# State-space layers of a perceiver block reordered along the next program's chain, one bias matmul of 256 columns, and a buffer cleared in two pieces elsewhere

## The reference, cut to what matters

```python
xz = x @ in_w
u, z = jnp.split(xz, 2, axis=-1)
uc = cb + sum((up[:, k:k + L, :] * cw[:, k] for k in range(D_CONV)))   # up: u padded in time
u = jax.nn.silu(uc)
proj = u @ xpw                       # dt (8), B (16), C (16)
delta = jax.nn.softplus(dt @ dtw + dtb)
h = exp(delta * A) * h + (delta * u) * B_t      # a scan over time, 16 states per channel
y = sum_n(h * C_t) + u * D
y = y * jax.nn.silu(z)
x = layer_norm(y @ ow + x)           # four layers, one after the other
```

## Time and profile before

| | us |
|---|---|
| median of 3 runs | 709.41 (709.27 to 709.52) |
| the profiled execution | 708.04 |
| its span, first to last instruction | 706.2 |
| busy in the span: TensorE, VectorE, ScalarE, POOL | 574.1, 478.9, 299.5, 161.7 |
| state-space layers, from the first turning (L1686) | 480.2 to 689 |

### The profile page before, as it was taken

How to read it: one execution, slowest core, us unless ns; L and a number is a source line. 1 busy time by engine, 2 the same in 40 slices (tenths; PEclk the granted TensorE clock), 3 DMA queues, 4 the chain that set the end, 5 groups by cost and what they waited for, 6 DMA issues and landing times.

```text
span 706.2 us, 21667 instructions
## 1 busy us (share of the span) xinstructions
PE 574.1 (81%) x8501; PEld 449.5 (64%) x8501; DVE 478.9 (68%) x1894; ACT 299.5 (42%) x851; POOL 161.7 (23%) x208
## 2 busy tenths in 40 slices
PE   3958758569995699999899999886788988898866
PEld 2625534357884688888888888875456656665634
DVE  1568649964444677777777777771588888978783
ACT  2868725224565333333233233233545444555411
POOL 2245533117000000000000000001564356336600
PEclk9989979796997555555555555555799999999997
DMA  8800000010002000000000000000000000000000
GB/s 341 354 1 2 1 3 1 2 41 3 1 1 90 3 3 0 0 0 0 0 0 0 0 0 0 0 1 0 1 0 1 1 0 1 1 0 1 1 0 7
DMA packets 6057, 15.26 MB, mean 22 GB/s; under 512 B 2641, under 2 KB 3289, under 8 KB 5505
## 3 DMA queue, kind: packets, MB, share of 16 engines
q1 hardware_dynamic: 5296, 11.19, 4.3%
q10 hardware_dynamic: 720, 3.55, 1.3%
HBM read 14.60 MB, written 0.13 MB: 21 GB/s over the span
## 4 chain that ended last, share of the span: by engine, by line
PE 41%; DVE 33%; ACT 13%; issue 10%; DMA 1%; DVEq 1%; POOL 0%; SPq 0%; ACTq 0%; POOLq 0%
PE bank L1678 9%; PE bank L1751 7%; PE bank L1587 6%; ACT esp L676 3%; PE bank L1538 2%; DVE ssum L1138 2%; ACT a L662 2%; DVE T L1208 2%; ACT e L678 2%; PE bank L1525 2%; DVE rz L1175 2%; DVE zs L1173 2%; DVE asp L1128 2%; DVE opre L1114 2%; ACT T L546 1%
## 5 line engine op out<-in xcount | busy, mean ns | idle before, releaser
L472 POOL MEMSET ctxT<- 128x128 f32 x1 | 0.3, 312 | 305.8 <-DVE xres L1182 305.8
L1587 PE MATMUL bank<-esp,qblk 128*128 128x1 f16 (+1 forms) x2048 | 66.5, 166 | 0.8 <-ACT esp L676 0.8
L1587 PE MATMUL bank<-hsp,kT 128*128 128x2 f16 x2048 | 63.5, 166 | 2.3 <-DVE hsp L1166 1.7
L1587 PEld LDWEIGHTS bank<-esp,qblk 128*128 128x128 f16 x2048 | 61.2, 104 | 1.4 <-ACT esp L676 1.1
L662 ACT ACTIVATE a<-opre 128x4 f32<-128x4 f32 x64 | 13.1, 205 | 115.2 <-DVE opre L1126 115.2
L1587 PEld LDWEIGHTS bank<-hsp,kT 128*128 128x128 f16 x2048 | 59.9, 104 | 3.1 <-DVE hsp L1163 1.7
L1208 DVE SCALAR_TENSOR_TENSOR T<-bank,bct,T 128x256 f32<-128x256 f32 x112 | 46.4, 476 | 1.3 <-PE bank L1764 1.3
L1195 DVE TENSOR_TENSOR_SCAN qblk<-ctxT,bank 128x512 f32<-128x512 f32 x32 | 37.6, 1208 | 13.2 <-PE bank L1751 13.2
L1587 PE MATMUL bank<-asp,lsp 128*128 128x4 f16 x768 | 30.7, 168 | 16.3 <-DVE asp L1128 16.3
L1195 DVE TENSOR_TENSOR_SCAN w<-kT,bank 128x512 f32<-128x512 f32 x32 | 37.6, 1208 | 8.4 <-PE bank L1751 8.4
L1587 PEld LDWEIGHTS bank<-asp,lsp 128*128 128x128 f16 x768 | 25.4, 105 | 27.8 <-DVE asp L1128 27.7
(11 more groups left out here) (326 smaller groups left out, 1410.5 us busy)
## 6 DMA issues: line engine op xcount, KB each, us to landing
w<-in_w_dram SPq DMA_DIRECT2D x2, 2048.0 KB
ctxT<-in_ctxT_dram SPq DMA_DIRECT2D x8, 256.0 KB, 13.4
wqkv<-in_qkvT_dram ACTq DMA_DIRECT2D x1, 1536.0 KB, 12.2
w<-in_mw_dram SPq DMA_DIRECT2D x1, 1024.0 KB, 5.1
lw<-in_lw_dram SPq DMA_DIRECT2D x1, 960.0 KB, 19.8
rows<-in_rows_dram ACTq DMA_DIRECT2D x1, 772.0 KB, 8.2
wqkv<-in_fw_dram SPq DMA_DIRECT2D x1, 532.0 KB, 3.4
T<-in_mask_dram ACTq DMA_DIRECT2D x1, 512.0 KB, 6.2
```

What stands on the lines that cost most here:

```text
L1587: return pe.matmul(out, lhsT, rhs, start=start, stop=stop, skip_group_check=True)
```

## The change

Four things. (1) POOL clears three quarters of `qblk` as its first instruction and the first quarter right after the cross-attention's last scaling, instead of all of it after L432; VectorE waits for both. (2) The two bias matmuls of 128 columns become one of 256 columns, at both places, and the one for the softplus' argument moves ahead of its input's wait. (3) The input projection is split: the u half goes before the convolution, the z half after it and after one bank of turned states; the sigmoid of u comes before that of z; the copy of bct moves behind the first exponential of the softplus; `turned_x` and the padded copy move ahead of the decays 5 to 7. (4) In each period, `sum_y` moves behind scan input 1, `project_out` between scan inputs 2 and 3, scan input 7 behind two banks of turned states; VectorE's scan 7 goes behind three read-outs and `gated_u`, and eight read-outs stand behind du instead of six; POOL waits for delta only, not for du.

```diff
--- POOL
+            pool.memset(qblk[:, 1:XG, :, :, :], 0.0).then_inc(sem["a_zero"], 1)
             pool.wait_ge(sem["d_mask"], 16)
...
             for i in range(B * XG):
...
+            pool.wait_ge(sem["x_max"], B * XG)
+            pool.memset(qblk[:, 0, :, :, :], 0.0).then_inc(sem["a_zero"], 1)
             pool.wait_ge(sem["a_wmean"], 1)
...
-            pool.memset(qblk[:, :, :, :, :], 0.0).then_inc(sem["a_zero"], 1)
...
-                pool.wait_ge(sem["m_delta"], 2 * c + 2)
+                pool.wait_ge(sem["m_delta"], 2 * c + 1)
--- ScalarE, prepare(c), new order
+                act.wait_ge(sem["m_uc"], c + 1)
+                step(act.activation(m_eu, bank[5][:, 0:TOK], ACT.Exp, scale=-1.0))
+                step(act.activation(m_lu, m_eu, ACT.Ln, bias=one))
+                act.activation(m_sg, m_lu, ACT.Exp, scale=-1.0).then_inc(sem["m_sig"], 1)
                 act.wait_ge(sem["m_uz"], 2 * c + 2)
                 step(act.activation(m_eu, bank[6][:, 0:TOK], ACT.Exp, scale=-1.0))
...
-                step.mark(act.activation(m_abs, bank[4][:, 0:TOK], ACT.Abs))
+                step(act.activation(m_abs, bank[4][:, 0:TOK], ACT.Abs))
                 act.wait_ge(sem["m_p"], 2 * c + 2)
+                step.mark(act.activation(bank[7][:, TOK:2 * TOK], m_abs, ACT.Exp, scale=-1.0))
                 act.activation(bct[:, s, :], bank[7][:, 0:2 * MN], ACT.Copy).then_inc(sem["m_bcs"], 1)
                 step.sync()
-                act.wait_ge(sem["m_bcs"], c + 1)
-                step(act.activation(bank[7][:, TOK:2 * TOK], m_abs, ACT.Exp, scale=-1.0))
--- ScalarE, period
                 decays(q, 0, 5)
                 if q >= 1:
                     rstd(q - 1)
-                decays(q, 5, 7)
                 if c:
                     turned_x(c)
-                decays(q, 7, NT)
+                decays(q, 5, 6)
+                if c:
+                    padded_u(c)
+                decays(q, 6, NT)
                 if c:
                     prepare(c)
--- VectorE
-                dve.wait_ge(sem["a_zero"], 1)
+                dve.wait_ge(sem["a_zero"], 2)
...
-                for i in range(3, NT):
+                for i in range(3, 7):
                     scan(q, i)
+                read_out(q, 0, 2)
                 if c:
                     gated_u(c)
+                read_out(q, 2, 3)
+                scan(q, 7)
+                if c:
                     gated_z(c)
-                read_out(q, 0, 7)
+                read_out(q, 3, 6)
                 if c:
                     ratio(c)
-                read_out(q, 7, 10)
+                read_out(q, 6, 8)
                 if c:
                     first_factor(c)
                     steps_of_time(c)
-                read_out(q, 10, MN)
+                read_out(q, 8, MN)
--- TensorE
-            def bias(to, n, start):
-                return mm(to, biasT[:, :], pat(cst[0:2 * ML * MC, C_ID + n:C_ID + n + 1], [[0, P]]), start=start)
+            def biases(to, n):
+                return mm(to[:, 0:TOK], biasT[:, :], pat(cst[0:2 * ML * MC, C_ID + n:C_ID + n + 1], [[1, MC], [0, P]]), start=True)
...
-                if q:
-                    scan_input(q, 0, 1)
-                    sum_y(q - 1)
-                    scan_input(q, 1, 4)
-                    project_out(q - 1)
-                else:
-                    scan_input(q, 0, 4)
-                scan_input(q, 4, 6)
+                scan_input(q, 0, 2)
+                if q:
+                    sum_y(q - 1)
+                scan_input(q, 2, 3)
+                if q:
+                    project_out(q - 1)
+                scan_input(q, 3, 6)
                 if c:
                     turned(c)
                 scan_input(q, 6, 7)
                 if c:
-                    project_in(c)
+                    project_in(c, 0)
                     convolve(c)
+                turn_state(q, 0, 1)
+                if c:
+                    biases(bank[4], ML * MC + c // 2 * MC)
+                    project_in(c, 1)
+                turn_state(q, 1, 2)
                 scan_input(q, 7, 8)
-                turn_state(q, 0, 2)
                 if c:
                     project_u(c)
                 turn_state(q, 2, 8)
```

More of the change, by code:

```diff
@@ L710, in turned_x, with padded_u @@
                 act.activation(m_xT[c % 2], bank[5][:, 0:P], ACT.Copy).then_inc(sem["m_xp"], 1)
+            def padded_u(c):
+                act.wait_ge(sem["m_uz"], 2 * c + 1)
+                act.activation(upad[:, c % 2, :, :, MK - 1:], bank[4][:, 0:TOK].rearrange("p (c b t) -> p c b t", c=MC, b=BT),
+                               ACT.Copy).then_inc(sem["m_up"], 1)
             def prepare(c):
                 s = c % 2
-                act.wait_ge(sem["m_uz"], 2 * c + 1)
-                act.activation(upad[:, s, :, :, MK - 1:], bank[4][:, 0:TOK].rearrange("p (c b t) -> p c b t", c=MC, b=BT),
-                               ACT.Copy).then_inc(sem["m_up"], 1)
+                act.wait_ge(sem["m_uc"], c + 1)
+                step(act.activation(m_eu, bank[5][:, 0:TOK], ACT.Exp, scale=-1.0))
+                step(act.activation(m_lu, m_eu, ACT.Ln, bias=one))
+                act.activation(m_sg, m_lu, ACT.Exp, scale=-1.0).then_inc(sem["m_sig"], 1)
                 act.wait_ge(sem["m_uz"], 2 * c + 2)
@@ L742, in _ @@
             turned_x(0)
+            padded_u(0)
             prepare(0)
@@ L1237, in gated_u @@
             def gated_u(c):
-                dve.wait_ge(sem["m_sig"], 2 * c + 2)
+                dve.wait_ge(sem["m_sig"], 2 * c + 1)
                 dve.tensor_tensor(m_gate_u[c % 2], bank[5][:, 0:TOK], m_sg, ALU.mult).then_inc(sem["m_uu"], 1)
             def gated_z(c):
-                dve.wait_ge(sem["m_sig"], 2 * c + 1)
+                dve.wait_ge(sem["m_sig"], 2 * c + 2)
                 dve.tensor_tensor(m_gate_z[c % 2], bank[6][:, 0:TOK], m_sz, ALU.mult)
@@ L1686, in turned, with project_in @@
                 pe.transpose(bank[5][:, 0:P], xn[:, c % 2, :], ident).then_inc(sem["m_xt"], 1)
-            def project_in(c):
+            def project_in(c, z):
                 l, s = divmod(c, 2)
                 pe.wait_ge(sem["m_xp"], c + 1)
[L1692 to L1697, removed]
-            def bias(to, n, start):
-                return mm(to, biasT[:, :], pat(cst[0:2 * ML * MC, C_ID + n:C_ID + n + 1], [[0, P]]), start=start)
+                for n in range(MC):
+                    at = (l * 2 * MC + z * MC + n) * P
+                    ins = mm(bank[6 if z else 4][:, n * P:(n + 1) * P], m_in[:, at:at + P], m_xT[s], start=(n == 0), stop=True)
+                ins.then_inc(sem["m_uz"], 1)
+            def biases(to, n):
+                return mm(to[:, 0:TOK], biasT[:, :], pat(cst[0:2 * ML * MC, C_ID + n:C_ID + n + 1], [[1, MC], [0, P]]), start=True)
             def convolve(c):
                 l, s = divmod(c, 2)
-                for ch in range(MC):
-                    bias(bank[5][:, ch * P:(ch + 1) * P], l * MC + ch, ch == 0)
+                biases(bank[5], l * MC)
                 pe.wait_ge(sem["m_up"], c + 1)
@@ L1718, in project_u @@
                 l, s = divmod(c, 2)
-                for to in range(MC):
-                    bias(bank[4][:, to * P:(to + 1) * P], ML * MC + l * MC + to, to == 0)
                 pe.wait_ge(sem["m_uu"], c + 1)
@@ L1795, in _ @@
             turned(0)
-            project_in(0)
+            project_in(0, 0)
             convolve(0)
+            biases(bank[4], ML * MC)
+            project_in(0, 1)
             project_u(0)
```

4 lines of the change are left out of this document (removed).

## The result

| | before | after |
|---|---|---|
| median of 4 runs each on one chip, us | 709.34 (708.71 to 709.52) | 696.31 (694.72 to 697.00) |
| the profiled execution, us | 708.04 | 696.79 |
| its span, us | 706.2 | 695.0 |
| granted clock, mean over the span | 0.748 | 0.756 |

The account below looks back on a forecast made before the run. The bound was one loop of waits from turn through projections, du, scans and residual to turn, with neither TensorE nor VectorE saturated. Terms -2.1-0.9-4.5-7.7=-15.2 took 708.04 to 692.8 us, 694.2 for the median; range 689 to 700.

Parts of the forecast that it names:

- The clearing: POOL's clearing of qblk, far from the periods, holds L798: 2.4 us saved, 0.3 lost to the second piece, sum -2.1.
- The preparation: Turn to du's end, seven inside the periods: 13.81 to 13.17 us, gain 0.64 each, together -4.5.
- 6.68: the projection starts there: Between turn and du: TensorE's queue lets project_u start 6.68 us after the turn, -0.51 instead of -1.1.
- The port: At du (L1265): du waits out POOL's fourth product, taking 0.6 us instead of 0.42 and ending near 13.17.
- The rivals in which one or two decays go ahead of du: At du, POOL's decays go first: one, 705.6 us, chance 0.10; two, 713.2 us, chance 0.05.
- The junctions: du's end to the next turn, seven times: -0.6 us each at half clock, -1.6 at full, together -7.7.
- residual at once: Behind scan 1, between du and the next turn: no wait, as the output projection is done at 6.5 us.
- half of seven to be spared: After du: half of the seven stretches to the next turn escape half clock, -7.7 us, bounds -4.2 and -11.2.
- never half clock: TensorE after du: full clock every time, seven stretches to the next turn give -11.2, total 690.7 us, chance 0.12.
- One sign of being wrong: Period of the state-space stage: the prediction is wrong if it stays above 23 us; 22.6 forecast at half clock.
- the rival of a half clock behind every du: TensorE after du: half clock every time, seven stretches to the next turn give -4.2, total 697.7 us, chance 0.20.
- The first preparation: Turn to du ahead of the periods: at half clock throughout (480 to 503 us), shortened by 0.9 us.

Follow-up runs that it names:

- the filler: The changed kernel plus three matmuls of 256 columns, result unused, in TensorE's wait before du is turned: 689.65 us, ratio 0.9730.

## Why the prediction was right

The total lay 2.1 us from the forecast, and part of that is luck. Between the two profiled executions, for which the sum was made, it is 4.0: forecast 692.8, measured 696.8; the 692.8 became 694.2 by the 1.4 us that the execution profiled before lay under its median, and the one profiled after lay 0.5 over its own. Those 4.0 are two terms that were too large, by 2.3 and 1.9. The other lines were off by up to 1.9 either way, and happen to add up to -0.2.

**The clearing** was right at its place: -2.4, and the scalings of lw did meet the addition, for 0.14 of the 0.3. What it is worth to the whole, 5.6 us alone, was not foreseen: the kernel behind it met other changes of the clock.

**The preparation** was the step that was mis-sized: "6.68: the projection starts there". It started at 554.95-547.87=7.08. Of the 0.40, the convolution began at 2.19 instead of 2.11 and took 1.89 instead of 1.78 (0.19), the first turned bank took 0.53 for 0.44, the z half 0.55 for 0.45, the biases 0.62 for 0.60. Four of the pieces between other pieces were a little short (the second turned bank and scan input 7 were exact), since I had taken tails off whole records; from start to start have the convolution at the same 1.89 (556.63 to 558.52). The kind of bound was right: the queue, with scan input 7 right ahead. The rest, from there to du's end, was 6.41, where 6.49 was forecast. So each preparation gave 0.31 instead of 0.64.

**The port** came out as written: du 0.64 (forecast 0.6), held by the fourth product, and next in line when it ended. The rivals in which one or two decays go ahead of du did not occur; with the decays' wait put back nothing changed. The Trainium skill (SBUF — State Buffer, "Who interferes with whom") agrees with the exclusion, and the runs show it in both directions: du 0.22 longer under a product, or eight decays 0.24 longer (8.05 against 7.81) when du is there first.

**The junctions** at either clock were near: 9.65 at half (forecast 9.44), 8.26 at full (8.45). At half clock the gate waited 1.30 for the sum of y (forecast 0.9), at full clock not. What shortens the junction is that the output projection went ahead of scan input 3, as the prediction's sum has it ("residual at once"). The count was off, and is the larger part of the 1.9: I had expected half of seven to be spared, and two were. That the phase moves was right, how far was a guess. With the filler, all of them are spared, which is the rival "never half clock" made to happen; it gave 689.65, where the prediction had 690.7, with a preparation that gave 2.3 us less and junctions that gave 1.5 more than its sum has. One sign of being wrong was half met: the period stayed above 23 where the clock fell (23.15, forecast 22.6), 0.32 of it the preparation and 0.21 the junction.

**Transposes and the clock.** By a rule of the Trainium skill (TensorE: Matmul & The Clock Gate, "Part 4: PE-mode transpose") the rival of a half clock behind every du would have been certain. From the last projection, at 556.4, to du's turning at 561.42 TensorE did turned states and waited, yet this du and one other were followed by full clock. So the rule does not make the half clock certain here. What tells the two from the five stays open.

**Left out.** The first preparation was not at half clock throughout (485.2 to 492.0 was granted 1.00): -2.0 for -0.9; with the old clearing, where it was, it took 16.7, -0.75. Of the +1.7 ahead of the clearing, 1.5 is the clock, and the +1.3 at the end lies wholly behind the state-space layers (18.5 us from their last normalisation to the end, 17.2 before), where the code is unchanged. I had costed the clock in the stage that was edited, and nowhere else.

What stays open: which changes of clock an execution meets outside the loop. The medians with ranges of 2 to 3 us in most runs are of this kind, and I have traces of one execution each.

## What to carry to other kernels

Where TensorE is granted the half clock behind a wait, first try work in that wait that nobody reads. Here three small matmuls per period gave 6.7 us, as much as half of the whole change, and eight more at the last wait stopped the half clock from taking the gains of the loop back, though they held the turning behind it back by 0.5 us. Then look at what already waits in the loop: the earlier trace rows show the residual waiting 0.94 us for the output projection, and moving that ahead of one scan input is what shortened the junction, 0.86 us at full clock. Read a term of the sum from record starts, not from lengths with a tail taken off, when the queue is the bound. And when an instruction is put ahead of another on one engine, follow what the one behind it releases: the exponential ahead of the bct copy won 0.23 us and lost 0.22 by sending POOL's products into du.

## What the runs showed of the hardware

- A VectorE instruction with two SBUF inputs that meets a POOL instruction waits for its end and goes next, even between POOL instructions that follow each other without a gap (0.64 us, then 0.42 once POOL was out of the way). Started 0.04 us ahead of POOL's, it runs undisturbed and POOL waits.
- A VectorE instruction with one tile and a column of scalars as its inputs (`oT<-oT,vec`) took 0.48 to 0.50 us under POOL's scalings in ten traces and 0.35 in four without them: longer, but not held until POOL's instruction ended (at 93.22, in the kernel after; it ended at 93.37).
- The same wait of TensorE, 1.65 us, was followed by 3.4 us of clock 0.50 five times and by 1.00 twice in one execution. With 1.46 us of matmuls in it, it was never followed by the half clock in six periods.
- The same code gets the half clock in other stretches from one execution to the next: up to the addition ahead of the second layer norm the kernel before and the same with unused matmuls in its loop are one program, and had it from 42.5 to 49.3 and from 39.8 to 53.4 us. With 2.4 us of wait removed (the clearing alone), the program was 4.0 to 7.2 us faster.
- A bias matmul with 16 rows costs by its columns: one of 256 took 0.62 us, two of 128 took 0.64.
